# Two PSUM banks instead of three for the projections and transposes of an attention stage, and a second one for the heads' context

## What is computed

```python
# x: (16, 256, 512) f32; 16 heads of 32; causal attention, biases on q, k, v and o
x = x + attn(layernorm(x), q_w, q_b, k_w, k_b, v_w, v_b, o_w, o_b)
x = x + xattn(ctx_2048, ctx_2048, layernorm(x), ssm_kernel, D, 8)   # convolution mixer over pairs
x = x + ffn(layernorm(x), w_gate_up, w_down)                        # 8-bit quantised values

def attn(x, ...):
    q, k, v = heads(x @ q_w.T + q_b), heads(x @ k_w.T + k_b), heads(x @ v_w.T + v_b)
    scores = einsum('bhqd,bhkd->bhqk', q, k) * SCALE, -inf above the diagonal
    return merge(einsum('bhqk,bhkd->bhqd', softmax(scores), v)) @ o_w.T + o_b
```

## Time and profile before

| | |
|---|---|
| median of 3 runs | 1251.77 us (1249.91 to 1253.16) |
| the profiled execution | 1254.34 us, span 1252.5 us |
| TensorE busy | 1142.7 us (91% of the span) |
| VectorE busy | 1004.7 us (80%) |
| ScalarE busy | 882.4 us (70%) |
| GpSimd busy | 963.2 us (77%) |
| mean granted TensorE clock | 0.957 |

### The profile page before, as it was taken

One profiled execution on the slowest core, in us unless ns is written; L12 is line 12 of the kernel. 1 busy time (PEld: TensorE's weight loads), 2 busy tenths in 40 slices (PEclk: granted clock), 3 DMA queues, 4 the chain that ended last, 5 costly groups with the idle time before them and its releaser, 6 DMA issues. The chain is left out here.

```text
span 1252.5 us, 33644 instructions
## 1 busy us (share of the span) xinstructions
PE 1142.7 (91%) x10082; PEld 814.2 (65%) x10082; DVE 1004.7 (80%) x3161; ACT 882.4 (70%) x1819; POOL 963.2 (77%) x1112
## 2 busy tenths in 40 slices
PE   5989999999999999997776999999999999999985
PEld 4767777777777777785344666666666666666642
DVE  4678888878788887887496888988988888888872
ACT  4678888878787888887372566667666666766654
POOL 1377787767777877786644999999999999999971
PEclk9979999999999999998766999999999999999996
DMA  6356655656555555555373433444333444433400
GB/s 204 96 167 196 219 176 162 185 166 189 192 176 179 160 167 179 171 174 161 146 280 95 141 98 131 139 142 138 125 112 131 134 142 142 130 114 124 124 25 26
DMA packets 87840, 186.57 MB, mean 149 GB/s; under 512 B 12176, under 2 KB 28816, under 8 KB 87760
## 3 DMA queue, kind: packets, MB, share of 16 engines
q1 hardware_dynamic: 86896, 185.02, 46.9%
q10 hardware_dynamic: 864, 0.66, 0.2%
HBM read 105.86 MB, written 54.61 MB: 128 GB/s over the span
## 5 line engine op out<-in xcount | busy, mean ns | idle before, releaser
L637 ACT ACTIVATE prob<-masked,negmax 128x128 f32<-128x128 f32 (+1 forms) x512 | 206.5, 455 | 67.2 <-DVE negmax L765 66.3
L765 DVE CUSTOM_DVE_ANT_0 masked<-s_ps,mask_f 128x128 f32<-128x128 f32 (+1 forms) x512 | 161.1, 352 | 33.7 <-PE s_ps L527 20.9
L1010 PE MATMUL y_ps<-kv,toep 128*128 128x288 f16 x640 | 184.7, 289 | 1.4 <-DVE prod L1346 1.4
L1011 PE MATMUL y_ps<-kv,toep 128*128 128x288 f16 x640 | 184.4, 288 | 0.0
L1012 PE MATMUL y_ps<-kv,toep 128*128 128x288 f16 x640 | 184.3, 288 | 0.0
L1066 PE MATMUL f_ps<-w1T,xiT 128*128 128x512 bf16 (+1 forms) x768 | 175.5, 365 | 0.9 <-ACT xiT L1187 0.7
L1194 ACT ACTIVATE silu<-gate,sx 128x512 f32<-128x512 f32 (+1 forms) x96 | 66.0, 688 | 139.9 <-DVE gate L1400 139.9
L1245 POOL TENSOR_TENSOR tree<-prod 128x512 f32<-128x512 f32 x128 | 163.1, 1274 | 1.3 <-DVE prod L1346 1.3
L406 POOL TENSOR_TENSOR kv_s<-kv_f,kv_s 128x1152 f16<-128x1152 f32 x64 | 152.3, 2379 | 0.6 <-ACT kv_s L651 0.6
L771 DVE TENSOR_TENSOR pT_lo<-t_ps,pT_hi 128x384 f16<-128x384 f32 x256 | 140.8, 550 | 11.4 <-ACT pT_hi L645 10.8
L645 ACT CAST pT_hi<-t_ps 128x384 f16<-128x384 f32 x256 | 122.5, 479 | 33.8 <-PE t_ps L536 32.7
(11 more groups left out here) (156 smaller groups left out, 3503.0 us busy)
## 6 DMA issues: line engine op xcount, KB each, us to landing
kv_pairs<-kv_s SPq DMA_DIRECT2D x64, 576.0 KB, 3.4
kv<-kv_pairs SPq DMA_DIRECT2D x32, 1152.0 KB, 8.2
c_in<-in_ctxr SPq DMA_DIRECT2D x64, 192.0 KB, 2.5
x_in<-in_x SPq DMA_DIRECT2D x16, 512.0 KB, 6.4
q_st<-q_hi SPq DMA_DIRECT2D x128, 64.0 KB, 2.0
k_st<-k_hi SPq DMA_DIRECT2D x128, 64.0 KB, 2.0
x_res<-in_x SPq DMA_DIRECT2D x16, 512.0 KB, 5.7
x_after_attention<-x_out SPq DMA_DIRECT2D x16, 512.0 KB, 4.3
```

Of the source, the lines that this page charges most:

```text
L637: ins = nc.scalar.activation(prob[h % 2][:, at:at + w], masked[h % 2][:, at:at + w], ACT.Exp, bias=negmax[:, h % 2, t:t + 1], scale=-1.0)
L765: ins = nc.vector.tensor_tensor_reduce(masked[h % 2][:, at:at + w], s_ps[h % 2][:, at:at + w], mask_f[:, S - w:S], -1.0, FAR, ALU.add, ALU ...
L1010: nc.tensor.matmul(dst, toep[p][:, 0, taps], c[:, 0, m], start=mt == 0, stop=False)
L1011: nc.tensor.matmul(dst, toep[p][:, 0, taps], c[:, 1, m], start=False, stop=False)
```

## The change

The rotation of the jobs has two banks instead of three: job n waits for job n - 2 to be emptied. The bank that this leaves becomes a second `o_ps`: four heads' contexts go to one, the next four to the other, and `values` waits for the division before the last one.

```diff
-G = 3
+G = 2
...
-    o_ps = ps("o_ps", [P, 512], F32)
+    o_ps = [ps(f"o_ps{p}", [P, 512], F32) for p in range(2)]
     g_ps = [ps(f"g_ps{p}", [P, 512], F32) for p in range(G)]
...
                 if h % HPT == 0:
 
-                    reached(pe, att_done, gn)
-                bank, head = o_ps, h % HPT * HPT + h // HPT
+                    reached(pe, att_done, gn - 1)
+                bank, head = o_ps[h // HPT % 2], h % HPT * HPT + h // HPT
...
                 dve.wait_ge(pv_done, (gn + 1) * HPT)
-                o = o_ps[:, 0:TT * HPT * VW].rearrange("p (t h c) -> p t h c", t=TT, h=HPT)
+                o = o_ps[g % 2][:, 0:TT * HPT * VW].rearrange("p (t h c) -> p t h c", t=TT, h=HPT)
```

## The result

The changed kernel takes 1307.31 us (median of 4 runs, 1303.4 to 1311.31), the kernel before 1251.58 in the same series: a ratio of 1.0436 (95% interval 1.0414 to 1.0458), 55.7 us more. The forecast was 1316, with a range from 1296 to 1336. The profile of the changed kernel was taken in the slowest of its four runs (1311.31 us).

The account below looks back on a forecast made before the run. TensorE was taken to bound the rounds. -1 (second context bank) + 47.1 (chain) + 1.9 (round 14) + 2.4 (ahead of the rounds) + 14 (clock) = 64.4 us on the 1251.77 median: 1316, range 1296 to 1336.

Parts of the forecast that it names:

- The bound: In the looped attention rounds TensorE sets the pace, busy 35.45 of 36 us; its waits are paid unless replacing later ones.
- The second context bank: TensorE's waits for the division of the context bank, 3.4 us at most, go away: 1 us of gain.
- The rival on the other side: The second context bank counts and job waits only replace waits for pT_lo: 1248 us; not slower has chance 0.03.
- The chain of a round: In rounds 1 to 13, late V0, V1 and O0 lengthen each round by 3.62 us, 47.1 us in all.
- the three waits: TensorE in each full round: V0 on QK3 1.61 us late, V1 on V0 idles 0.74, O0 on X0 idles 2.07.
- O1: O1 on X1, the fourth tight pair of a full round: no wait, margin 0.13 us, bounds 0 and 0.5.
- The clock: After O0's wait TensorE's clock falls for some 3.4 us in 8 rounds of 13: 14 us, bounds 0 and 22.
- Ahead of the rounds: Before the rounds V0 is 2.2 us late and the last X about 1.1: 2.4 us taken, bounds 0 and 5.
- Rounds 13 to 15: Round 13 has the full chain, round 14 only the first two waits (1.9 us), round 15 no tight pair.
- my own case: Waits, with the clock down in part or all of the rounds at O0: 1316 us, range 1306 to 1328, chance 0.55.
- Waits only: Rival: the job waits come without clock loss, 1302 us, range 1297 to 1306, chance 0.23.
- Falls at V0 too: Rival: clock loss at V0 and O0 in every round, 1346 us, range 1328 to 1350, chance 0.10.
- Partly absorbed: Rival: ScalarE or VectorE catches up so that O0 hardly waits, 1280 us, range 1265 to 1297, chance 0.09.

Follow-up runs that it names:

- the filled kernel: Two job banks and one context bank, plus six matmuls whose result nothing reads ahead of O0's wait in rounds 1 to 13: 1302.09 us, ratio 1.0401 to the kernel before.
- the two other kernels with all three waits: Against the kernel before: two job banks with one context bank, 1306.33 us; three job banks with each job waiting for job n - 2, 1303.93 us.
- O0 alone: Kernel before, three job banks, only O0 of each round waits for the job two before (X0): 1296.88 us, ratio 1.0360.
- V1 alone: Kernel before, three job banks, only V1 of each round waits for the job two before (V0): 1276.18 us, ratio 1.0191.

## Why the prediction held, point by point

**The bound.** Right: TensorE's order sets the pace of the rounds, and what it waits is paid. The single waits show the exception that the prediction named: a new wait is repaid where an old one follows it.

**The second context bank, 1 us gain.** Not contradicted, and not shown: without it 1306.33 against 1307.31, with wide overlap, and a gain of 1 us can't be told from none. The rival on the other side is out.

**The chain of a round, 3.62 us.** Measured 3.70 over a trip of the loop. Each of the three waits came at its place and with its releaser. A listed wait counts from the modelled end of the matmul before, which lies 0.17 us behind the time at which the next could have been issued (an A job's row is 0.60 long, the next issue comes after 0.43). With that added the rows say 1.62, 0.84 and 1.93 us, against 1.61, 0.74 and 2.07 worked out. O1 did not wait, despite a margin of 0.13.

**The clock, 14 us.** The place was right, shown by the filled kernel. The size was not: five falls of 13 in the profile (three and two in the two other kernels with all three waits), where I took eight. Each made a round of 38.75 us 40.3 long, some 1.6 us more, so 8 us in this profile, and 3 to 4 by the medians with and without the filling. The granted clock of the loop, 0.98 to 0.99, is at or above the upper end of the 0.93 to 0.98 that I had said. I had read ten waits of ten as nearly a rule. With dense matmuls on either side a wait of this size made the clock fall only sometimes: O0 alone, 2.4 us long, four times in 13, V1 alone, 1.8 to 2.1 us long, seven in 13. And the length alone does not decide: V0's wait in the changed kernel is 1.75 us as well, in every second round from round 4 on, five times, and no fall followed one of them; nor did one for 9 us follow this wait of V0 ahead of the rounds:

```profile
31.16 0.38 PE L465 MATMUL g_ps<-wv_hi,xT_hi 128*128 128x512 f16 x1 [2.13 <-DVE k_lo L737]
```

Why O0 and not V0, and why in these rounds and not in others, no run here tells.
The Trainium skill (TensorE: Matmul & The Clock Gate, "A second HAM failure mode: psum-queue depth-cycling") let tiny idles between groups of matmuls make the clock swing. The runs agree only for some waits of 1.75 us and more; with waits of 0.5 to 1.7 us left in each round, the filled kernel kept 1.00.

**Ahead of the rounds, 2.4 us.** The statistics of round 0 come 2.67 us later than before, as worked out; by round 1 only 0.58 of it is left. In the kernel before the clock was low for 13.7 us in round 0, in the changed one for 10.2: that would give 1.7 us back. But the kernel with three banks and the wait of two had 10.2 us at the lower level there as well, and was 2.76 us late by round 1, so why so little is left here is open.

**Rounds 13 to 15.** From round 13's statistics to the last output 4.2 us were added, where 3.6 for O0's chain, 1.6 for one fall and 1.9 for round 14 were due: some 3 us are missing. I had let nothing be absorbed there. Round 15, whose TensorE waits on others anyway, may have absorbed them; but the clock was also low for less time behind round 13's fall, 13.7 us instead of 20.5 in the kernel before, worth up to 3.4 us. The two are not told apart. The end of the attention in both kernels, the one before first (length, TensorE's busy us, clock):

```profile
540.00:622.80 82.80, 69.11 (x707) 0.88 0.48 158
```

```profile
595.00:679.50 84.50, 70.34 (x731) 0.92 0.44 151
```

The sum: 0.6 ahead, 44.4 in twelve rounds, 6.4 for four falls in them, 4.2 behind make 55.6, of 57.0 us between the two spans; about 1.1 of the rest lies in early rounds and stays unexplained. Against the forecast's 64.4 us the clock term is the one that was sized wrong (14 for 8), followed by the waits ahead of the rounds (2.4 for 0.6) and the last rounds; all three were too high, and the chain of a round, which is most of the sum, was right to 0.1 us. The median lies only 1.3 us above the lower end of the range that I had given to my own case (1306 to 1328).

**The rivals.** Waits only (1302) was nearer in the number than my own case (1316), and a run without a fall is what the filled kernel shows; but the falls are there. Falls at V0 too: out. Partly absorbed: out for the loop, open for the last rounds.

## What to carry to other kernels

With work in a hand-written order, the depth of a rotation costs nothing until a buffer's next user starts earlier than its emptying ends; list for each user the distance to the one n places back, and the tight pairs can be costed from one timeline, by following the emptying engines' queues in order. A bank given to a place where nobody waits was worth nothing here, however much it looks like double buffering: look for the wait's row first. Before an instruction is moved forward into idle steps, check when its input lands, in the first rounds too: the steady rounds hide a queue that is late once.

## What the runs showed of the hardware

A wait of TensorE of 1.8 to 2.4 us amid dense matmuls was followed by a fall of the granted clock from 2.4 to 1.2 GHz for 3.4 us in some rounds and not in others (five of 13 at 1.8 us, four of 13 at 2.4, seven of 13 at 1.8 to 2.1), and V0's waits of 1.75 us by none in five. Six matmuls whose result nothing reads, put into the O0 wait of 1.8 us, left no fall in rounds 1 to 13, where there had been three, and the added work cost no time (1302.09 against 1306.33 us). The eight banks' use itself left no mark: two banks in rotation or three with the waits of two gave 1.0425 and 1.0420.
